# Turning and splitting the third CIN weight inside the main loop, and taking the last CIN step in rounded high and low parts, in two halves of the batch

## The reference

```
e  = rows of 39 tables by ids                       # [512, 39, 16]
X1 = einsum('hjk,bjd,bkd->bhd', W0, e, e)  + b0     # h = 128
X2 = einsum('hjk,bjd,bkd->bhd', W1, e, X1) + b1
X3 = einsum('hjk,bjd,bkd->bhd', W2, e, X2) + b2
z  = concat(X1.sum(d), X2.sum(d), X3.sum(d))        # [512, 384]
h  = relu(concat(z, dense_ctx) @ W_top1 + b_top1)   # 512 wide
h  = relu(h @ W_top2 + b_top2)                      # 256 wide
y  = h @ W_top3                                     # [512, 1]
```

## Time and profile before

| what | us |
|---|---|
| median of three runs (lowest, highest) | 709.32 (709.06, 712.4) |
| the profiled execution | 708.21 |
| its span, first to last instruction | 706.4 |
| TensorE busy | 673.8 |
| ScalarE busy | 546.4 |
| VectorE busy | 476.2 |
| GpSimd busy | 454.9 |

### The profile page before, as it was taken

The page is one execution under the profiler, slowest core; times in us unless marked ns, Lnnn a source line. Parts: engine busy times, 40 slices in busy tenths (PEclk is TensorE's granted clock), DMA queues, the critical chain, the costliest instruction groups (busy, mean ns, idle before and its releaser), DMA issues. The chain is left out here.

```text
span 706.4 us, 10134 instructions
## 1 busy us (share of the span) xinstructions
PE 673.8 (95%) x2647; PEld 484.4 (69%) x2647; DVE 476.2 (67%) x928; ACT 546.4 (77%) x1958; POOL 454.9 (64%) x445
## 2 busy tenths in 40 slices
PE   4478899999999999999999999999999999999998
PEld 4266667777777777777777777777777777776443
DVE  3256777777787778778777777777877777887000
ACT  3346788888898888988888889888988898998003
POOL 6516847777878787877887878777877555322000
PEclk9669899999999999999999999999999999999999
DMA  8244131312131312212121313131313140300000
GB/s 294 59 165 145 9 95 5 95 6 94 6 95 7 94 8 70 31 47 54 30 71 15 85 7 94 6 94 8 95 6 95 5 158 10 143 5 0 1 0 0
DMA packets 99163, 40.77 MB, mean 58 GB/s; under 512 B 80593, under 2 KB 84957, under 8 KB 98850
## 3 DMA queue, kind: packets, MB, share of 16 engines
q1 hardware_dynamic: 93059, 37.58, 20.2%
q0 software_dynamic: 5120, 1.29, 2.1%
q10 hardware_dynamic: 927, 1.26, 0.6%
HBM read 11.26 MB, written 2.56 MB: 20 GB/s over the span
## 5 line engine op out<-in xcount | busy, mean ns | idle before, releaser
L508 ACT ACTIVATE prod<-ps_y,xt 128x128 f32<-128x128 f32 x1792 | 493.9, 435 | 79.0 <-PE ps_y L831 64.5
L829 PE MATMUL ps_y<-w_hi,x_hi 128*128 128x512 f32 (+1 forms) x640 | 312.0, 488 | 6.4 <-ACT prod L508 3.6
L830 PE MATMUL ps_y<-w_lo,x_hi 128*128 128x512 f32 (+1 forms) x640 | 249.7, 390 | 0.0
L831 PE MATMUL ps_y<-w_hi,x_lo 128*128 128x512 f32 (+1 forms) x640 | 249.3, 390 | 0.0
L369 POOL TENSOR_TENSOR prod<-prod 128x512 f32<-128x512 f32 x120 | 155.1, 1292 | 114.0 <-ACT prod L508 107.1
L679 DVE SCALAR_TENSOR_TENSOR prod<-ps_y,xt,prod 128x128 f32<-128x128 f32 x576 | 164.6, 344 | 55.2 <-PE ps_y L831 47.8
L340 POOL DMA_INDIRECT rows<-in_table,index x160 | 155.5, 972 | 39.1 <-issue 32.9
L829 PEld LDWEIGHTS ps_y<-w_hi,x_hi 128*128 128x128 f32 x640 | 120.8, 189 | 67.0 <-issue 23.9
L686 DVE TENSOR_REDUCE prod<-prod 128x128 f32<-128x1536 f32 (+1 forms) x64 | 116.3, 1818 | 60.1 <-ACT prod L508 60.1
L830 PEld LDWEIGHTS ps_y<-w_lo,x_hi 128*128 128x128 f32 x640 | 121.1, 189 | 47.5 <-issue 23.9
L364 POOL TENSOR_TENSOR room<-room 117x512 f32<-117x512 f32 (+1 forms) x105 | 135.3, 1292 | 14.7 <-DMA room<-room 14.7
(11 more groups left out here) (99 smaller groups left out, 245.6 us busy)
## 6 DMA issues: line engine op xcount, KB each, us to landing
room<-room SPq DMA_DIRECT2D x75, 234.0 KB
room<-room SPq DMA_DIRECT2D x45, 78.0 KB
emb_room<-rows SPq DMA_DIRECT2D x168, 5.0 KB
rows<-in_table,index POOLq DMA_INDIRECT x160
w2t_dram<-g_all SPq DMA_DIRECT2D x1, 2496.0 KB, 9.1
room<-w2t_dram SPq DMA_DIRECT2D x1, 2496.0 KB, 9.2
room<-room SPq DMA_DIRECT2D x15, 156.0 KB
g_all<-in_L_rec_W SPq DMA_DIRECT2D x9, 256.0 KB
```

Of the source, the lines that this page charges most:

```text
L508: ins = nc.scalar.activation(prod[:, SLOT[k] + m // 2, :, m % 2], ps_y[:, g % YBANKS, m * H:(m + 1) * H], ACT.Copy, scale=xt[:, q % 2, ti, ...
L829: nc.tensor.matmul(y, hi, w1_hi[:, cols], start=True, stop=False)
L830: nc.tensor.matmul(y, hi, w1_lo[:, cols], start=False, stop=False)
L831: nc.tensor.matmul(y, lo, w1_hi[:, cols], start=False, stop=True).then_inc(y_made, 1)
```

## The change

W2's ten turns leave the start; the ring of the other turns gets two more banks. W2 is loaded in five parts during quads 1 to 5 (SP's list) into rows of `g_all` that the second half of the batch fills later. In ten tiles (the last of one quad and the first of the next, from tile 7 to tile 24) TensorE turns a group of four fields into `ps_tr`, ScalarE keeps it rounded, VectorE its remainder; SP stores both parts to DRAM. During the last tile SP loads them back over `w1_hi` and `w1_lo`. All known parts of MLP layer 1 are taken per half of the batch, and none in the last quad. Layer 2 goes in 2 x 20 steps of two fields and 256 columns: ScalarE makes G's high part, VectorE the low part, in a ring of four, and TensorE makes three products a field. The first half's MLP is put between steps of the second half.

```diff
-TURNS = ([("w2", g) for g in range(GROUPS)] + [("w1", g) for g in range(4)] + [("w0", 0), ("w0", 1)]
-         + [("w1", g) for g in range(4, GROUPS)] + [("dense", 0)])
+TURNS = ([("w1", g) for g in range(4)] + [("w0", 0), ("w0", 1)] + [("w1", g) for g in range(4, GROUPS)]
+         + [("dense", 0)])
+PREP_BANKS = YBANKS + 2
...
+W2_SIZE = 4
+W2_GROUPS = -(-F // W2_SIZE)
+W2_PARTS = W2_GROUPS // 2
+W2_TURNED_IN = {QT * (n // 2 + 1 + n % 2) + (0 if n % 2 else 3): n for n in range(W2_GROUPS)}
+W2_TURNED_AFTER = 4
+W2_SAVED_BEHIND = 4
...
+HALF = B // 2
+PAIR = 2
+STEPS = -(-F // PAIR)
+RING = 4
+H1_AFTER, H2_AFTER, OUT_AFTER = STEPS + 3, STEPS + 8, STEPS + 13
...
-        ps_r3 = ps_y[:, 2, :]
-        ps_h2 = [ps_y[:, 3, :], ps_y[:, 4, :]]
+        ps_r3 = [ps_y[:, 2, 0:HALF], ps_y[:, 4, 0:HALF]]
+        ps_h2 = [[ps_y[:, 3, 0:HALF], ps_y[:, 3, HALF:]], [ps_y[:, 2, 0:HALF], ps_y[:, 3, 0:HALF]]]
...
-        w2t = room[:, 0:F * H]
+        w2_hi, w2_lo = w1_hi, w1_lo
...
+        g_hi = sb("g_hi", [P, RING, PAIR * HALF], F32R)
+        g_lo = [x[:, par, :] for par in range(2) for x in (x1_hi, x1_lo)]
...
+                if q <= W2_PARTS:
+                    if q == 1:
+                        sp.wait_ge(prep_tr, len(TURNS))
+                    load_w2(q - 1)
+                if 0 <= q - W2_SAVED_BEHIND < W2_PARTS:
+                    save_w2(q - W2_SAVED_BEHIND)
...
-            sp.wait_ge(w2_saved, 16)
-            sp.wait_ge(z_used, CHUNKS * QUADS)
-            sp.wait_ge(xt_turned, QUADS)
-            sp.dma_start(w2t, w2t_dram).then_inc(late_w2, 16)
-            sp.wait_ge(y_out, 1)
-            sp.dma_start(out.rearrange("b a -> a b"), y_row[0:1, :]).then_inc(stored, 16)
-            sp.wait_ge(stored, 16)
+            sp.wait_ge(w2_saved, 32 * W2_PARTS)
+            for n in range(GROUPS // 2):
+                sp.wait_ge(y_made, GROUPS * (TILES - 1) + 2 * n + 2)
+                cols = slice(FIRST[2 * n] * H, (FIRST[2 * n + 1] + SIZES[2 * n + 1]) * H)
+                for low, dst in enumerate((w2_hi, w2_lo)):
+                    sp.dma_start(dst[:, cols].bitcast(F32), w2_dram[low][:, cols]).then_inc(late_w2[n], 16)
...
+                    if g == 6 and T in W2_TURNED_IN:
+                        n = W2_TURNED_IN[T]
+                        act.wait_ge(w2_turned, n + 1)
+                        nc.scalar.copy(w2_home(False, n).bitcast(F32R),
+                                       ps_tr[:].rearrange("p (r c) -> p r c", c=HALF)).then_inc(w2_hi_made, 1)
+            def high_part(u):
+                half, first = u // STEPS, u % STEPS * PAIR
+                n = min(PAIR, F - first)
+                wait(act, g_used, u - RING + 1)
+                nc.scalar.copy(g_hi[:, u % RING, 0:n * HALF].rearrange("p (j b) -> p j b", b=HALF),
+                               g_all[:, first:first + n, HALF * half:HALF * (half + 1)]).then_inc(g_hi_made, 1)
+            def keep_r3(half):
...
+            for u in range(2 * STEPS):
+                if u == RING:
+                    keep_g(TILES - 1)
+                if u == H1_AFTER + 1:
+                    keep_r3(0)
+                high_part(u)
+                if u == H1_AFTER + RING:
+                    keep_h1(0)
+                if u == H2_AFTER + RING:
+                    keep_h2(0)
+                if u == OUT_AFTER + RING:
+                    keep_y(0)
+            keep_r3(1)
+            keep_h1(1)
+            keep_h2(1)
+            keep_y(1)
...
+                if T in W2_TURNED_IN:
+                    n = W2_TURNED_IN[T]
+                    dve.wait_ge(w2_hi_made, n + 1)
+                    nc.vector.tensor_tensor(w2_home(True, n).bitcast(F32R),
+                                            ps_tr[:].rearrange("p (r c) -> p r c", c=HALF),
+                                            w2_home(False, n), ALU.subtract).then_inc(w2_lo_made, 1)
...
+            for u in range(2 * STEPS):
+                half, first = u // STEPS, u % STEPS * PAIR
+                n = min(PAIR, F - first)
+                if u < RING:
+                    dve.wait_ge(y_made, GROUPS * (TILES - (QT if u < 2 else 0)))
+                dve.wait_ge(g_hi_made, u + 1)
+                nc.vector.tensor_tensor(g_lo[u % RING][:, 0:n * HALF].rearrange("p (j b) -> p j b", b=HALF),
+                                        g_all[:, first:first + n, HALF * half:HALF * (half + 1)],
+                                        g_hi[:, u % RING, 0:n * HALF].bitcast(F32).rearrange("p (j b) -> p j b", b=HALF),
+                                        ALU.subtract).then_inc(g_lo_made, 1)
...
+                wait(pe, w2_lo_made, sum(T <= QT * (q - 1) for T in W2_TURNED_IN))
...
+            def turn_w2(T):
+                n = W2_TURNED_IN[T]
+                if n % 2 == 0:
+                    pe.wait_ge(w2_ld[n // 2], 16 if n // 2 < W2_PARTS - 1 else 32)
+                pe.wait_ge(x0_made, T // QT + 3 if n % 2 == 0 else T // QT + 2)
+                wait(pe, w2_lo_made, n)
+                src = w2_home(True, n)
+                for m in range(min(W2_SIZE, F - W2_SIZE * n)):
+                    ins = nc.tensor.transpose(ps_tr[:, m * H:(m + 1) * H],
+                                              src[:, m // 2, m % 2 * H:(m % 2 + 1) * H], ident[:])
+                ins.then_inc(w2_turned, 1)
...
+            def known_mlp1(half):
+                n = slice(HALF * half, HALF * (half + 1))
+                pe.wait_ge(late_mlp, 16 * 6)
+                pe.wait_ge(r1_done, 1)
+                if half == 1:
+                    pe.wait_ge(g_kept, TILES)
+                    pe.wait_ge(h1_made, MC1)
+                for m in range(MC1):
+                    nc.tensor.matmul(ps_h1[m][:, n], wt1[0:C, 3, m * P:(m + 1) * P], dense_t[:, n], start=True, stop=False)
+                    for part, z in ((0, r1), (1, g_all[:, F, :])):
+                        nc.tensor.matmul(ps_h1[m][:, n], wt1[:, part, m * P:(m + 1) * P], z[:, n], start=False, stop=False)
...
-                    if not nxt and (ti, g) in MLP_AFTER:
-                        known_mlp1(*MLP_AFTER[ti, g])
-            for m in range(2, MC1):
-                if m == 2:
-                    pe.wait_ge(dve_step, DVE_STEPS * (TILES - 1) + DVE_DONE[YBANKS])
-                else:
-                    pe.wait_ge(act_step, ACT_STEPS * (TILES - 1) + ACT_GROUPS.index(YBANKS + 1) + 1)
-                for part in range(2):
-                    known_mlp1(m, part)
+            pe.wait_ge(dve_step, DVE_STEPS * (TILES - 1) + DVE_DONE[YBANKS])
+            pe.wait_ge(act_step, ACT_STEPS * (TILES - 1) + ACT_GROUPS.index(YBANKS + 1) + 1)
+            known_mlp1(0)
...
+            for u in range(2 * STEPS):
+                half, first = u // STEPS, u % STEPS * PAIR
+                pe.wait_ge(g_lo_made, u + 1)
+                for j in range(first, min(first + PAIR, F)):
+                    if half == 0:
+                        part = next(n for n in range(GROUPS // 2) if j < FIRST[2 * n + 1] + SIZES[2 * n + 1])
+                        pe.wait_ge(late_w2[part], 32)
+                    hi = g_hi[:, u % RING, (j - first) * HALF:(j - first + 1) * HALF]
+                    lo = g_lo[u % RING][:, (j - first) * HALF:(j - first + 1) * HALF]
+                    w_hi, w_lo = w2_hi[:, j * H:(j + 1) * H], w2_lo[:, j * H:(j + 1) * H]
+                    nc.tensor.matmul(ps_r3[half], w_hi, hi, start=j == 0, stop=False)
+                    nc.tensor.matmul(ps_r3[half], w_lo, hi, start=False, stop=False)
+                    ins = nc.tensor.matmul(ps_r3[half], w_hi, lo, start=False, stop=j == F - 1)
+                ins.then_inc(g_used, 1)
+                if u == H1_AFTER:
+                    r3_part(0)
+                if u == H2_AFTER:
+                    pe.wait_ge(h1_made, MC1)
+                    for m in range(MC2):
+                        for c in range(MC1):
+                            ins = mlp2_product(0, c, m)
                         ins.then_inc(h2_summed, 1)
-            for m in range(MC2):
-                pe.wait_ge(h2_made, m + 1)
-                ins = nc.tensor.matmul(ps_out, wt3[:, m:m + 1], h2[:, m, :], start=m == 0, stop=m == MC2 - 1)
-            ins.then_inc(y_summed, 1)
+                if u == OUT_AFTER:
+                    mlp3(0)
+                    known_mlp1(1)
+            r3_part(1)
+            for c in range(MC1):
+                pe.wait_ge(h1_made, MC1 + c + 1)
+                for m in range(MC2):
+                    ins = mlp2_product(1, c, m)
+                    if c == MC1 - 1:
+                        ins.then_inc(h2_summed, 1)
+            mlp3(1)
```

150 lines of the change are left out of this document (82 added, 68 removed).

## The result

| | kernel before | changed kernel |
|---|---|---|
| median of seven runs each (lowest, highest), us | 710.45 (709.06, 712.97) | 704.24 (700.58, 704.72) |
| ratio, 95% interval | | 0.9897 [0.9871, 0.9923] |
| the profiled execution, its span, us | 708.21, 706.4 | 704.72, 702.9 |

The change makes the kernel 6.2 us faster (forecast 10.9). The two profiled executions lie only 3.5 us apart: before's is shorter than all seven of its kernel, after's is the longest of its seven. What follows divides those 3.5 us.

What follows compares the result with a forecast made beforehand. TensorE, busy 95% of the span, was taken as the bound. Start -12.2, turns +5.5, last quad -1.8 and end -2.4 sum to -10.9 us on 706.4: span 695.5, median 698.5 (own range 694 to 702; overall 690 to 709).

Steps and rivals of the forecast that it cites:

- the turns: W2 turned in ten tiles of quads 1 to 6: 0.55 us of TensorE time each, 5.5 us added.
- the last quad: Loses 3.4 us of MLP products but cannot shrink under ScalarE's 32.18 us: 1.8 us gained; sign: it takes 32.4 us.
- the middle quad: Sign of being right: a middle quad with two turns of W2 takes 37.9 us.
- layer 2's distance: Sign of being right: layer 2's products of 256 columns are 0.117 us apart.
- the first product: Sign of being right: the first layer 1 product comes at 34 to 38 us; before, at 48.20 us.
- the end: Behind the loop, layer 2 and the halved MLP: 54.4 us against 56.8, 2.4 us gained; sign: 54 to 55 us.
- The start: With W2 out of the start, the first layer 1 product comes earlier: 12.2 us gained.
- the bounds: Limits of the gain at the start, 7.7 us if all handovers are held and 16.8 us if none; middle taken.
- held signals: Rival: the train of gathers holds TensorE's signals to its end, start gains 7.7 us: 703 us, chance 0.20.
- 12 products of two passes, 5.2 us: Known MLP products ahead of layer 2, behind the loop, each pass of 256 columns at 0.215 us.
- weights bound layer 2: Rival: weight loads of 0.189 us set layer 2's pace, 16.9 us more: 715.5 us, chance 0.08.
- exposed turns: Rival: ScalarE and VectorE hold a bank at each W2 turn, 18.5 instead of 5.5 us: 711.5 us, chance 0.08.

Runs made afterwards that it cites:

- e4: The changed kernel without any work on W2 (no loads, turns, stores or reload), on a quick chip (kernel before 689.08 us): 682.65 us, ratio 0.9905.
- e7: The changed kernel, unchanged, run again on a slow chip (kernel before 712.06 us): 702.99 us, ratio 0.9860.
- e6: The kernel before, unchanged, run again on a slow chip: 711.86 us, ratio 1.0006.
- e5: The changed kernel with MLP layer 1's known products reordered, the four 16-row products first, on a slow chip: 701.01 us, ratio 0.9845 to the kernel before.
- e3: The kernel before with only W2's turns, loads and store taken out of the start, on a quick chip: 685.05 us, ratio 0.9949.
- e12: The changed kernel with grouped MLP products and pauses in the gathers of quads 1 to 3, on a slow chip: 693.81 us, ratio 0.9748 to the kernel before.
- e10: The kernel before with pauses in the gathers of quads 1 to 3 and nothing else, on a quick chip: 692.62 us, ratio 1.0049.
- e9: The changed kernel with grouped MLP products and pauses in the gathers of quads 1 to 3, on a quick chip: 689.45 us, ratio 0.9997 to the kernel before.

## Why the prediction was right, and where it was not

The sign and the range held; the size was 4.7 us too large in the medians, 7.4 us between the profiled executions. There was luck in it. Three terms promised 11.5 us too much, and two, the turns and the last quad, 4.4 us too little; without these two the time would have been near 709, the range's upper end. Of the five signs of being right, the middle quad (37.7 us, forecast 37.9) and layer 2's distance came; the first product, the last quad (30.7, forecast 32.4) and the end (56.7, forecast 54 to 55) lay outside.

**The start, -12.2 forecast, -9.9 measured.** The mechanism held in part. The chain from regrouping lay in the train of gathers and took 16.8 us instead of 11.4. But what started it was not gather 0's rows, as forecast: VectorE was already regrouping them at 20.05 us, while ScalarE still waited for the last two turns, 1.67 and 1.56 us "remote", and began at 21.57 us (forecast 20) right behind them. The hold reached the weights too, for which the sum had no term; on the quick chip, in e4, it was the rows ("DMA rows" in the bracket at 19.23). My window for the first product was 34 to 38 us; it came at 38.34. The hold cost 5.35 us in the chain and 1.57 ahead of it, 6.9 of the 9.1 us between the bounds, where I took the middle, 4.6. One reading behind it was loose. The timeline also has

```profile
29.26 0.59 ACT L466 COPY w0t<-ps_y 117x512 f32<-117x512 f32 x1 [3.61 <-remote]
```

so ScalarE had gone on before the train's last gather was issued (29.39), and 32.80 us was not the end of the hold.

**What the sum did not have: quads 0 and 1, +5.1 and +2.15 us** (0.4 of it the turn in quad 1). This is the step that failed: I let the gain at the first product pass through to the end. An earlier first product meets the later trains elsewhere, and they hold signals too. By tiles: quad 0's first takes 15.36 us instead of 13.14 (TensorE, which had idled 3.70 us in its start, has its clock at the 1.2 GHz level for the first nine products, where before's was already up), its second 14.58 instead of 13.44, its last 11.38 instead of 9.25, and quad 1's first 12.97 instead of 11.15; e7 against e6 gives the same four, 1.4, 1.1, 2.0 and 1.7 us. The last two fit the windows of quad 2, for which GpSimd waits behind quad 3's train, changed kernel, then before:

```profile
92.22 1.30 POOL L418 TENSOR_TENSOR room<-room 117x512 f32<-117x512 f32 x1 [8.69 <-DMA room<-room]
```

```profile
94.91 1.29 POOL L364 TENSOR_TENSOR room<-room 117x512 f32<-117x512 f32 x1 [3.20 <-DMA room<-room]
```

TensorE turned quad 2's rows at 80.47 us and ScalarE copied them at 87.39, 6.9 us later; in before's trace 2.8 us lie between (87.34, 90.11). By the end of quad 1 only 2.6 us of 9.9 are left (132.83 against 135.43), while in e5's luckier execution, with the same code up to there, all of it is (125.06). The rival "held signals" named the mechanism and its 703 is nearer to 704.24 than my 698.5, but it too put the whole price ahead of the first product.

**The turns, +5.5 forecast.** 0.42 us each on undisturbed chips, so 4.2 for ten: my nearest row was the one of 0.46, and I should have stayed with it. On the first chip quads 2 to 6 grew by 2.34 us only, because before's own quad 2 was disturbed (its last tile 9.14 us, 8.2 to 8.4 in the quads around it) and most of its first tiles took 10.1 us where a quick chip has 9.91. Nothing was exposed: between 100 and 600 us TensorE's products wait once, 1.5 us for GpSimd, and its weight loads at most 0.6 us for ScalarE or VectorE.

**The last quad, -1.8 forecast, -3.5 measured.** I took ScalarE's 32.18 busy us as a floor. As many instructions were busy 30.73 us afterwards, 100% of the quad. Instructions that follow each other without a wait overlap in part: twelve take 3.21 us and four 1.15 (rows above), 0.27 against 0.29 us each. So each wait for TensorE had lengthened "busy" as well; that this is all of the 1.4 us is not shown. All 3.4 us of TensorE work came off.

**The end, -2.4 forecast, 0.0 measured.** Layer 2's distance was right (0.118 against 0.117 us); the tail behind it took 9.3 us (forecast 9.9). What was mis-sized is the term "12 products of two passes, 5.2 us": 6.65 us, twice, since every block changes from 16 rows of weights to 128 and back. The earlier trace rows had the warning: 4.21 us for eight passes of the known parts is 0.53 each, where layer 2's 78 take 0.43. Grouped, the end is 54.4 us, the forecast's number to the tenth by luck: a grouped call takes 5.5 us, not 5.2, and the shorter tail made it up. The rivals "weights bound layer 2" and "exposed turns" fell. 256 columns alone are 0.107 us at 2.4 GHz, each product had its own weights over all rows, and they started 0.118 us apart. The trace does not agree with the rule of the Trainium skill by which a weight load overlaps products only in another row group; it stands in "TensorE: Matmul & The Clock Gate", section "The mechanism", not in the section that the prediction names.

From the forecast to the profiled executions: -10.9 + 2.3 (start) + 6.8 (quads 0 and 1 without the turn) - 2.7 (turns, as that trace has them) + 0.3 (quads 7 to 14) - 1.7 (last quad) + 2.4 (end) = -3.5 us.

**What the change is worth elsewhere.** On a quick chip: start -4.0, last quad and the small rest -2.4 (e4 against e3), turns +4.2: about -2.2 us of 689, an estimate, since the changed kernel itself was never run there. The version that beats both on slow chips is e12 (0.975 of before, against 0.986 and 0.990 for the changed kernel); what pacing would give the kernel before there was not measured, since e10 ran on a quick chip; on a quick chip its twin e9 is level with the kernel before, and e5, by sum 684.6 us, would be better there.

## What to carry to other kernels

Work pulled out from behind a serial start gains only what the stages behind it can use: before crediting it, walk the same stretch of the trace with every later resource (next trains of gathers, the clock, the next rows) at its new time. Do not take an engine's busy time in a stretch as its floor when another engine feeds it. Keep products of one weight height together, and time a kernel whose start is bound by many small gathers on more than one chip before believing a gain of a per cent.
